# State-space preparation: pass 0's softplus in SBUF, the rests of the inputs on GpSimd, a wait of its own for each pass

## The reference

```python
xd = einsum('bdl,kd->blk', x, xw)
dts, Bs, Cs = xd[..., :8], xd[..., 8:24], xd[..., 24:]
delta = softplus(einsum('blr,dr->bld', dts, dtw) + dtb)
A = -exp(Al)
dA = exp(delta[..., None] * A)
dBx = delta[..., None] * Bs[:, :, None, :] * xt[..., None]
h = h * dA + dBx                      # along l, for each channel and each of 16 states
y = sum over the states of h * C, + xt * Dv, layer norm
```

## Time and profile before

| | us |
|---|---|
| median of 3 executions | 5132.19 |
| lowest and highest | 5129.77, 5133.94 |
| the profiled execution: its time | 5128.04 |
| the profiled execution: its span in the trace | 5126.2 |
| mean granted TensorE clock in the span | 0.868 of full |

### The profile page before, as it was taken

How to read it: one execution, slowest core, us unless ns; L and a number is a source line. 1 busy time by engine, 2 the same in 40 slices (tenths; PEclk the granted TensorE clock), 3 DMA queues, 4 the chain that set the end, 5 groups by cost and what they waited for, 6 DMA issues and landing times.

```text
span 5126.2 us, 46896 instructions
## 1 busy us (share of the span) xinstructions
PE 4178.4 (82%) x17450; PEld 1981.5 (39%) x17450; DVE 3659.2 (71%) x4992; ACT 2119.7 (41%) x2567; POOL 2008.9 (39%) x681
## 2 busy tenths in 40 slices
PE   5699966999669996699966989679896798967988
PEld 2254422444224442344323444234442344423443
DVE  6865778657786578775787757877668775787766
ACT  4234542335424354243542435424354243542435
POOL 3531535415354053440534505445054450544505
PEclk7699977999779997799977999779997799977999
DMA  1020100211002100021000210002200022000120
GB/s 38 0 59 14 37 9 1 59 25 26 9 0 59 31 21 9 3 57 38 14 8 9 51 43 9 9 9 50 50 1 9 9 50 50 1 9 9 42 50 9
DMA packets 62966, 125.91 MB, mean 25 GB/s; under 512 B 18825, under 2 KB 21001, under 8 KB 62482
## 3 DMA queue, kind: packets, MB, share of 16 engines
q1 hardware_dynamic: 62738, 122.91, 10.4%
HBM read 12.23 MB, written 8.39 MB: 4 GB/s over the span
## 4 chain that ended last, share of the span: by engine, by line
PE 49%; DVE 23%; issue 10%; SPq 6%; ACT 6%; POOL 3%; DMA 2%; DVEq 0%; ACTq 0%; POOLq 0%
PE PS L1400 9%; PE PS L1348 9%; PE PS L1295 8%; PE PS L1127 6%; SPq L305 3%; DVE work L850 3%; DVE work L852 3%; DVE mx L959 3%; PE PS L1186 3%; PE PS L1102 3%; PE PS L1224 3%; PE PS L1439 2%; SPq L295 2%; DMA QS<-nm 2%; POOL work L398 1%
## 5 line engine op out<-in xcount | busy, mean ns | idle before, releaser
L959 DVE TENSOR_REDUCE mx<-PS 128x1 f32<-128x512 f32 x2048 | 1278.8, 683 | 414.8 <-PE PS L1295 414.2
L628 ACT ACTIVATE PT<-PS 128x1024 f32<-128x1024 f32 x1024 | 1000.5, 1022 | 855.8 <-PE PS L1400 833.1
L414 POOL TENSOR_TENSOR piece<-PT 128x2048 f32<-128x2048 f32 x48 | 220.2, 4588 | 1885.5 <-ACT PT L628 1885.5
L1295 PE MATMUL PS<-KS,QS 96*128 96x512 f32 x2048 | 840.5, 469 | 65.0 <-DVE mx L959 29.4
L414 POOL TENSOR_TENSOR piece<-piece,PT 128x2048 f32<-128x2048 f32 x192 | 879.8, 4582 | 15.4 <-ACT PT L628 0.5
L394 POOL TENSOR_TENSOR work<-work,Crep 128x1024 f32<-128x1024 f32 x256 | 615.9, 2407 | 389.5 <-DVE work L850 191.6
L1400 PE MATMUL PS<-QS,KS 98*128 98x512 f32 x2048 | 673.0, 420 | 42.7 <-DMA QS<-nm 42.4
L1295 PEld LDWEIGHTS PS<-KS,QS 96*128 96x128 f32 x2048 | 374.5, 197 | 561.7 <-DVE mx L959 402.4
L1224 PE MATMUL PS<-dstk,sel 128*128 128x512 f32 (+1 forms) x640 | 317.3, 571 | 319.2 <-DVE work L852 127.9
L1348 PE MATMUL PS<-PT,Vt 128*32 128x512 f32 x4096 | 547.1, 606 | 25.3 <-DVE oT L983 18.8
L548 ACT ACTIVATE PS<-PS,Aneg 128x1024 f32<-128x1024 f32 x256 | 278.3, 1087 | 626.2 <-PE PS L1224 595.5
(11 more groups left out here) (205 smaller groups left out, 5135.4 us busy)
## 6 DMA issues: line engine op xcount, KB each, us to landing
QS<-piece SPq DMA_DIRECT2D x384, 128.0 KB, 2.4
KS<-piece SPq DMA_DIRECT2D x384, 128.0 KB, 2.4
xin<-x SPq DMA_DIRECT2D x8, 1024.0 KB
out<-xr SPq DMA_DIRECT2D x8, 1024.0 KB, 4.0
W<-wpack SPq DMA_DIRECT2D x2, 1024.0 KB
QS<-nm SPq DMA_DIRECT2D x128, 8.0 KB, 1.9
W<-wpack SPq DMA_DIRECT2D x1, 576.0 KB
W<-wpack SPq DMA_DIRECT2D x2, 256.0 KB
```

What stands on the lines that cost most here:

```text
L414: pool.tensor_tensor(total, first, PT[:, i % PT_RING, :, :], ALU.add).then_inc(sum_pool.sem, 1)
L628: act.activation(PT[:, i % PT_RING, 2 * pr:2 * pr + 2, :], PS[:, 2 + 2 * pr:4 + 2 * pr, :], ACT.Exp, scale=SCALE).then_inc(p_sb.sem, 1)
L959: dve.tensor_reduce(mx[:, at, cc:cc + 1], PS[:, row_slot(n, cc), :], AX.X, ALU.max).then_inc(r_max.sem, 1)
L1295: pe.matmul(PS[:, row_slot(n, cc), :], QS[0:kd, c, h, q * P:q * P + P], KS[0:kd, h, cc * N:cc * N + N], start=True, stop=True).then_inc(r_ ...
```

## The change

GpSimd's `sample` gets the rests of pass 0's step and of pass 2's input. Pass 0's decay is written to the SBUF row `yv[:, 2, :]` instead of PSUM, and all that follows in pass 0 reads and writes there. VectorE's waits in `below` and `steps` are taken apart. The waits for all rests ahead of the scan go from ScalarE and VectorE. TensorE waits for GpSimd's rests at the start of each pass (4, 6, 8 of 8) and for VectorE's four (passes 1 and 2) ahead of scan step 1, whose `dstk` matmul writes to banks 6 and 7. Its pass 2 coefficients wait for pass 0's decay and no longer for `rests(0)`.

```diff
+        u_of = lambda ps: yv[:, 2, :] if ps == 0 else dl_of(ps)
...
-        rests_in = sig("rests_in", 8)
-        rests_pool = sig("rests_pool", 4)
+        rests_in = sig("rests_in", 4)
+        rests_pool = sig("rests_pool", 8)
...
             def sample(b):
-                for ps in range(2):
+                halves_of = [(slice(64 * hh, 64 * hh + 64), slice(64 - 64 * hh, 128 - 64 * hh)) for hh in range(2)]
+                pool.wait_ge(*heads_d(b, 2))
+                for hh, (r, ro) in enumerate(halves_of):
+                    pool.tensor_tensor(dstk[ro, hh, 0:L], u_of(0)[r, :], dstk[r, hh, 0:L].bitcast(F32),
+                                       ALU.subtract).then_inc(rests_pool.sem, 1)
+                for ps in range(3):
                     at, w = PASS_AT[ps], PASS_W[ps]
                     pool.wait_ge(*heads_u(b, 2 * ps + 2))
-                    for hh in range(2):
-                        r, ro = slice(64 * hh, 64 * hh + 64), slice(64 - 64 * hh, 128 - 64 * hh)
+                    for hh, (r, ro) in enumerate(halves_of):
                         pool.tensor_tensor(ustk[ro, hh, at:at + w], ux_of(ps)[r, :], ustk[r, hh, at:at + w].bitcast(F32),
                                            ALU.subtract).then_inc(rests_pool.sem, 1)
...
                     if n == 0:
-                        pool.wait_ge(*rests_pool(b, 4))
+                        pool.wait_ge(*rests_pool(b, 8))
...
-                    act.activation(dl_of(ps), dl_of(ps), ACT.Exp, scale=-1.0).then_inc(sp_exp.sem, 1)
+                    act.activation(u_of(ps), dl_of(ps), ACT.Exp, scale=-1.0).then_inc(sp_exp.sem, 1)
...
-                act.wait_ge(*rests_in(b, 8))
-                act.wait_ge(*rests_pool(b, 4))
...
                 def below(ps):
-                    poly, dl = poly_of(ps), dl_of(ps)
+                    poly, u = poly_of(ps), u_of(ps)
+                    dve.wait_ge(*sp_exp(b, ps + 1))
+                    if ps > 0:
+                        dve.wait_ge(*sp_ln(b, ps + 1))
+                    dve.tensor_scalar(small_of(ps), u, SMALL_U, None, ALU.is_lt).then_inc(sp_small.sem, 1)
                     dve.wait_ge(*sp_q(b, ps + 1))
-                    dve.wait_ge(*sp_one(b, ps + 1))
-                    dve.wait_ge(*sp_ln(b, ps + 1))
-                    dve.tensor_scalar(small_of(ps), dl, SMALL_U, None, ALU.is_lt).then_inc(sp_small.sem, 1)
-                    dve.tensor_tensor(poly, poly, dl, ALU.mult).then_inc(sp_qu.sem, 1)
+                    dve.tensor_tensor(poly, poly, u, ALU.mult).then_inc(sp_qu.sem, 1)
...
                 below(0)
                 steps(0)
                 below(1)
-                rests(0)
                 steps(1)
                 below(2)
                 steps(2)
                 rests(1)
                 rests(2)
-                dve.wait_ge(*heads_u(b, 6))
-                for hh in range(2):
-                    r, ro = slice(64 * hh, 64 * hh + 64), slice(64 - 64 * hh, 128 - 64 * hh)
-                    dve.tensor_tensor(ustk[ro, hh, PASS_AT[2]:COLS], ux_of(2)[r, :], ustk[r, hh, PASS_AT[2]:COLS].bitcast(F32),
-                                      ALU.subtract).then_inc(rests_in.sem, 1)
...
-                dve.wait_ge(*rests_pool(b, 4))
...
-                pe.wait_ge(*rests_in(b, 2))
+                pe.wait_ge(*sp_exp(b, 1))
...
+                    if n == 1:
+                        pe.wait_ge(*rests_in(b, 4))
                     if n % SG == 0:
-                        pe.wait_ge(*rests_in(b, (2, 4, 8)[ps]))
-                        pe.wait_ge(*rests_pool(b, (2, 4, 4)[ps]))
+                        pe.wait_ge(*rests_pool(b, (4, 6, 8)[ps]))
```

More of the change, by code:

```diff
@@ L461, in decayed @@
                     act.wait_ge(*sp_abs(b, n_parts[ps]))
-                    act.activation(dl_of(ps), dl_of(ps), ACT.Exp, scale=-1.0).then_inc(sp_exp.sem, 1)
+                    act.activation(u_of(ps), dl_of(ps), ACT.Exp, scale=-1.0).then_inc(sp_exp.sem, 1)
                 def quadratic(ps):
                     act.wait_ge(*sp_exp(b, ps + 1))
-                    act.activation(poly_of(ps), dl_of(ps), ACT.Identity, scale=1.0 / 3, bias=mhalf[:, :]).then_inc(sp_q.sem, 1)
+                    act.activation(poly_of(ps), u_of(ps), ACT.Identity, scale=1.0 / 3, bias=mhalf[:, :]).then_inc(sp_q.sem, 1)
                 def logarithm(ps):
-                    act.activation(one_of(ps), dl_of(ps), ACT.Identity, bias=1.0).then_inc(sp_one.sem, 1)
-                    act.activation(ln_of(ps), dl_of(ps), ACT.Ln, bias=1.0).then_inc(sp_ln.sem, 1)
+                    act.activation(one_of(ps), u_of(ps), ACT.Identity, bias=1.0).then_inc(sp_one.sem, 1)
+                    act.activation(ln_of(ps), u_of(ps), ACT.Ln, bias=1.0).then_inc(sp_ln.sem, 1)
                 def coefficient(ps, dst, src_ps, done, bank):
@@ L482, in head_of_step @@
                         r = slice(64 * hh, 64 * hh + 64)
-                        act.activation(dstk[r, hh, at:at + w], dl_of(ps)[r, :], ACT.Copy).then_inc(heads_d.sem, 1)
+                        act.activation(dstk[r, hh, at:at + w], u_of(ps)[r, :], ACT.Copy).then_inc(heads_d.sem, 1)
                 def head_of_input(ps):
@@ L751, in below, with steps @@
                 def below(ps):
-                    poly, dl = poly_of(ps), dl_of(ps)
-                    dve.wait_ge(*sp_q(b, ps + 1))
-                    dve.wait_ge(*sp_one(b, ps + 1))
-                    dve.wait_ge(*sp_ln(b, ps + 1))
-                    dve.tensor_scalar(small_of(ps), dl, SMALL_U, None, ALU.is_lt).then_inc(sp_small.sem, 1)
-                    dve.tensor_tensor(poly, poly, dl, ALU.mult).then_inc(sp_qu.sem, 1)
[L760 to L766, removed]
+                    poly, u = poly_of(ps), u_of(ps)
[3 more added lines that the diff above has]
+                    dve.tensor_scalar(small_of(ps), u, SMALL_U, None, ALU.is_lt).then_inc(sp_small.sem, 1)
+                    dve.wait_ge(*sp_q(b, ps + 1))
+                    dve.tensor_tensor(poly, poly, u, ALU.mult).then_inc(sp_qu.sem, 1)
+                def steps(ps):
+                    poly, u, ux = poly_of(ps), u_of(ps), ux_of(ps)
+                    dl = cut = u
+                    if ps == 0:
+                        cut = one_of(0)
+                    dve.wait_ge(*sp_qu(b, ps + 1))
+                    dve.scalar_tensor_tensor(out=poly, in0=poly, scalar=1.0, in1=u, op0=ALU.add,
+                                             op1=ALU.mult).then_inc(sp_poly.sem, 1)
+                    dve.wait_ge(*sp_one(b, ps + 1))
+                    dve.scalar_tensor_tensor(out=cut, in0=one_of(ps), scalar=-1.0, in1=u, op0=ALU.add,
                                              op1=ALU.subtract).then_inc(sp_cut.sem, 1)
                     dve.wait_ge(*sp_cut(b, ps + 1))
-                    dve.tensor_tensor(dl, ln_of(ps), dl, ALU.subtract).then_inc(sp_sum.sem, 1)
+                    dve.wait_ge(*sp_ln(b, ps + 1))
+                    dve.tensor_tensor(dl, ln_of(ps), cut, ALU.subtract).then_inc(sp_sum.sem, 1)
                     dve.wait_ge(*sp_small(b, ps + 1))
@@ L788, in rests @@
                         r, ro = slice(64 * hh, 64 * hh + 64), slice(64 - 64 * hh, 128 - 64 * hh)
-                        dve.tensor_tensor(dstk[ro, hh, at:at + w], dl_of(ps)[r, :], dstk[r, hh, at:at + w].bitcast(F32),
+                        dve.tensor_tensor(dstk[ro, hh, at:at + w], u_of(ps)[r, :], dstk[r, hh, at:at + w].bitcast(F32),
                                           ALU.subtract).then_inc(rests_in.sem, 1)
```

## The result

The changed kernel took 5087.7 us (median of 4 executions, 5079.3 to 5089.6), the kernel before, beside it, 5131.0 (4 executions, 5126.3 to 5133.9). The ratio is 0.9915, 95% interval 0.9899 to 0.993: 43 us less, between 36 and 52. The forecast was 5093 from the earlier median of 5132.2, which is 39 less.

A forecast was written before the change was run, and what follows sets the result against it. The prediction took VectorE's 33.7 us path in each of eight preparations as the bound. Shortening each by 4.9 us saves 39 us, from the median 5132.2 to 5093, range 5085 to 5118.

The forecast's parts named there:

- Pass 0: VectorE's preparation: the mask waits for the exponential, not the logarithm; product starts 3.2 us earlier, at 681.45 to 681.6.
- Pass 1 and the collision: VectorE's `copy_predicated` waits for GpSimd's subtraction, both reading SBUF; some 2.7 us long, pass ends at 703.1.
- The undecided point: Whether VectorE or GpSimd goes next between two ready GpSimd subtractions; pass 1's end bounded by 701.6 and 707.9.
- the main case: VectorE gets in at the next border between GpSimd subtractions; preparation 4.9 us shorter, 5093 us; chance 0.80.
- Pass 2: ScalarE's logarithm sets VectorE's start, covering 1.4 us of GpSimd's delay; first scan product 4.9 us earlier (4.75 to 5.0).
- the 0.95 end of that term: ScalarE's Silu behind its table load moves up by 0.73 to 0.95 us; pass 2's logarithm ends at 704.5 to 704.7.
- The scan's start: GpSimd's last two rests take 0.74 to 1.54 us each; its queue keeps 0.8 us to spare before its first product.
- The sum: Whole kernel: 8 preparations by 4.9 us is 39 us, taken from the median 5132.2 to give 5093.
- B: VectorE's pass 1 copy gets in only when GpSimd pauses; pass ends at 707.9, time 5118 us; chance 0.10.
- C: TensorE's clock stays low in the scan; some 10 more 1 us waits a sample, 5173 us; chance 0.03.
- D: The gain is met by another wait later in the sample, such as a transfer; 5132 us; chance 0.04.

The follow-up runs named there:

- the run with two more masks: Changed kernel with VectorE's mask of pass 1 computed three times (2.5 us more work): preparation 39.15 us, 5096.2 us in one execution.
- the copy without a collision: Changed kernel with GpSimd's first rest also waiting until pass 1's `copy_predicated` is over: preparation 39.92 us, 5087.7 us in one execution.
- the other order: Changed kernel with pass 2's parts ahead of the Silu on ScalarE and its matmuls ahead of z on TensorE: preparation 36.71 us, 5066.5 us.
- the second time: The changed kernel, unaltered, measured again beside the kernel before: 5088.4 us against 5126.2, ratio 0.9917.

## Why the prediction was right

**Pass 0.** The mask started 3.2 us before the logarithm of pass 0 ended, and the product at 678.57, which in the clock of the forecast (2.91 us later, by the start of f1) is 681.48; I had 681.45 to 681.6. The mask in SBUF took 0.70 (0.79 to 1.22 forecast), the quadratic from SBUF 1.15 (1.11 to 1.24). Writing the exponential to SBUF cost nothing: 1.03 us for L467, as for L462 in the earlier trace rows, against what the Trainium skill's rule on destinations might suggest (ScalarE: Activation LUTs, Step-by-step: what each stage is for). One small term was off: `copy_predicated` with all operands in SBUF took 1.36, not 1.23.

**Pass 1 and the collision.** The wait ahead of the mask was 1.39 (1.5 forecast), the copy 2.73 us (2.7), the pass's end 700.31, or 703.22 in the forecast's clock (703.1). The undecided point, who is next at a border, went as the main case had it, and the run with two more masks shows it inside a pair. GpSimd's subtraction behind it was held up by 0.85 us, where I had 1.2. The rule of the Trainium skill (SBUF — State Buffer, SBUF: two separate sides), a lock for a whole instruction, agrees with all of these rows: each blocked copy began its own 0.50 or 1.23 us within 0.2 us of the end of a GpSimd instruction (696.48 here, with the first pair's end at 696.62).

**Pass 2.** ScalarE set its start, and the collision was hidden by it: shown by the copy without a collision (pass 2's mask no earlier) and by the other order (1.43 gained). The table load went ahead of the end of the z matmuls (694.91 against 695.14), so the 0.95 end of that term was the right one, or a little more: pass 2's logarithm came 1.0 us earlier, and pass 2's mask, at 701.62, 0.2 us earlier than I had it. In the sample on which I worked the first product therefore came 5.1 us earlier (43.24 to 38.13), outside my 4.75 to 5.0. That sample was one of the two long ones; in most samples the gain is 4.82, and over all eight 4.85 on average. That this meets the forecast of 4.9 so closely is in part luck: the mask's 0.2 us and the 0.3 us by which the sample was longer than most cancel nearly.

**The scan's start.** GpSimd's last rests ended at 712.95, and the two of 320 columns took 0.90 each (0.74 to 1.54 forecast). They delayed nothing.

**The sum.** 38.8 us in the preparations against 39. The total follows it only because the rest of the run stayed nearly as long: 4782.0 us outside the preparations before, 4779.4 after. In the profiles of the experiments, where only the preparation is changed further, this part is up to 12.5 us shorter or 5 us longer than that. My range had 4 us for it, which was too little; that the total came out at 43 (38 the second time) against 39 is luck to that extent.

**The rivals.** B (entry only in a pause) is refuted: pass 1's copy took 2.73 us, and B needs over 6. C (the clock low through the scan) did not come: VectorE waited 86 times for the spread, 88.1 us, where the earlier trace rows has 88 times and 87.7. D (met by another wait) did not come either: the span is shorter by 41.4 us, all of the 38.8 and more.

## What to carry to other kernels

When one engine's unbroken row of work is thinned, the next engine's queue becomes the bound quickly: 3.2 us gained in pass 0 and 2.5 us of rests taken off VectorE shortened the preparation by 0.95 and 0.80 us, and a mere change of order on ScalarE and TensorE was then worth 1.43. Work moved to GpSimd is free where GpSimd idles, but it holds up VectorE instructions with two SBUF inputs for the rest of its instruction; look whether a wait of VectorE follows that covers it. Judge a small change by the length of its own stage in the profile, where it repeats to 0.03 us in most samples, beside the total, which here strayed from plain addition by 3 to 16 us.

## What the runs showed of the hardware

- A VectorE `copy_predicated` that waits for GpSimd gets in between two GpSimd instructions that are both ready (begun by 697.70 in a pair that lasted from 695.49 to 701.12), and makes the next one 0.85 us longer, two thirds of its own 1.23. None of the 118 blocked ones waited for a second GpSimd instruction, also where one was ready (79 of them).
- The same mask takes 0.70 us from SBUF to SBUF and 1.23 from PSUM for 1024 columns; `copy_predicated` takes 1.36 within SBUF and 1.23 into PSUM.
- Equal work in the scan took 57.1 or 59.9 us within one execution, with granted clocks of 0.76 and 0.72.
